# Spare bf16 products on constants between TensorE's steps, in two front ends and in the tail

## The reference, cut to what matters

```python
mod = (_silu(L0_c) @ L0_wmod).reshape(L0_c.shape[0], 6, 1, -1)
h = _layernorm(x) * (1 + ca) + sa
x = x + ga * _L0_attn_ref(h, ...)
h = _layernorm(x) * (1 + cb) + sb
x = x + gb * _L0_ffn_ref(h, ...)
# inside _L0_attn_ref, per pair of names:
scores = (relu(x @ modr_w1 + modr_b1) @ modr_w2 + modr_b2)      # top 128 of the 256 tokens, in order
n1 = _ln(tok);  uv = n1 @ m_in_w;  u, res = halves of uv         # a gated mix
tok = tok + (u * s * silu(res)) @ m_out_w
n2 = _ln(tok);  logits = n2 @ moe_r_w + moe_r_b                  # top 2 of 8 experts
h1 = gelu(n2 @ moe_w1[e] + moe_b1[e]);  eo = h1 @ moe_w2[e] + moe_b2[e]
# inside _L0_ffn_ref: both operands of each product are rounded to 8 magnitudes in blocks of 16
h = silu(fp4_linear(x, w_gate)) * fp4_linear(x, w_up);  out = fp4_linear(h, w_down)
```

## Time and profile before

| | |
|---|---|
| median of 3 runs | 287.74 us (287.31 to 289.43) |
| the profiled execution's own time | 289.48 us |
| its span, first to last instruction | 287.8 us |
| mean clock granted to TensorE over the span | 0.788 of full |
| busy: PE, PEld, DVE, ACT, POOL | 186.8, 149.6, 182.0, 111.2, 104.5 us |
| DMA | 30.74 MB, 107 GB/s in the mean |

### The profile page before, as it was taken

One profiled execution on the slowest core, in us unless ns is written; L12 is line 12 of the kernel. 1 busy time (PEld: TensorE's weight loads), 2 busy tenths in 40 slices (PEclk: granted clock), 3 DMA queues, 4 the chain that ended last, 5 costly groups with the idle time before them and its releaser, 6 DMA issues.

```text
span 287.8 us, 3751 instructions
## 1 busy us (share of the span) xinstructions
PE 186.8 (65%) x1079; PEld 149.6 (52%) x1079; DVE 182.0 (63%) x569; ACT 111.2 (39%) x321; POOL 104.5 (36%) x120
## 2 busy tenths in 40 slices
PE   2574578893337599887999679399798560083630
PEld 1321563742336469776578667298777460041530
DVE  0994856277887845693498466998568216879510
ACT  2426213143502264860457456446556400022210
POOL 6400037110641871057011615845304378300370
PEclk9957595786559597996699999989999875559575
DMA  7920002000117940466139564628284021000000
GB/s 214 331 76 0 0 2 55 18 1 1 36 61 274 370 131 2 146 187 202 54 85 292 189 216 130 192 94 259 67 282 127 28 56 46 9 0 0 2 27 9
DMA packets 22964, 30.74 MB, mean 107 GB/s; under 512 B 2128, under 2 KB 16792, under 8 KB 22944
## 3 DMA queue, kind: packets, MB, share of 16 engines
q1 hardware_dynamic: 20896, 26.30, 29.0%
q0 software_dynamic: 2048, 4.20, 4.8%
HBM read 24.45 MB, written 6.05 MB: 106 GB/s over the span
## 4 chain that ended last, share of the span: by engine, by line
PE 36%; DVE 27%; POOL 11%; issue 9%; ACT 9%; DMA 3%; SPq 1%; DVEq 0%; ACTq 0%; POOLq 0%
PE aux_ps L1083 20%; PE moe_ps L1083 7%; POOL ys L498 3%; POOL hx L466 3%; ACT hT L590 3%; POOL xs_dram L491 3%; PE small_ps L1083 2%; DVE q_am L757 2%; DMA hx<-x_dram 2%; PE aux_ps L1284 2%; DVE stats L726 2%; DVE hh L1055 2%; DVE hh L1051 1%; DVE qa L771 1%; PE aux_ps L1110 1%
## 5 line engine op out<-in xcount | busy, mean ns | idle before, releaser
L654 ACT ACTIVATE h1T<-moe_ps,w_e 128x128 f32<-128x128 f32 x120 | 33.9, 375 | 12.7 <-PE moe_ps L1083 10.3
L1083 PE MATMUL moe_ps<-xsT,w_e 128*128 128x128 f32 x240 | 32.8, 282 | 7.0 <-issue 6.7
L1083 PEld LDWEIGHTS moe_ps<-xsT,w_e 128*128 128x128 f32 x240 | 30.0, 196 | 9.1 <-issue 8.3
L1083 PE MATMUL moe_ps<-w_e,h1T 128*128 128x128 f32 x240 | 33.7, 289 | 1.7 <-ACT h1T L654 1.7
L1083 PEld LDWEIGHTS moe_ps<-w_e,h1T 128*128 128x128 f32 x240 | 30.8, 201 | 3.7 <-ACT h1T L654 2.5
L477 POOL TENSOR_TENSOR rstd<-veps,half_pow 128x4 f32<-128x4 f32 (+2 forms) x11 | 12.3, 1116 | 52.1 <-DVE veps L731 51.9
L491 POOL DMA_INDIRECT xs_dram<-xd,slot_ix x16 | 16.1, 1005 | 26.7 <-DVE slot_ix L987 22.4
L466 POOL TENSOR_TENSOR hx<-qa,q_sc 128x704 f32<-128x704 f32 (+2 forms) x6 | 7.5, 1255 | 44.3 <-DVE qa L772 44.3
L1051 DVE SCALAR_TENSOR_TENSOR hh<-gth,aux_ps 128x352 f32<-128x352 f32 x16 | 8.3, 519 | 17.4 <-ACT gth L692 17.3
L1284 PE MATMUL aux_ps<-ident,hx 128*128 128x128 f32 (+1 forms) x48 | 9.6, 354 | 14.4 <-POOL hx L466 14.4
L498 POOL DMA_INDIRECT ys<-ys_dram,slot_ix x16 | 15.9, 993 | 7.5 <-issue 4.1
(11 more groups left out here) (218 smaller groups left out, 442.5 us busy)
## 6 DMA issues: line engine op xcount, KB each, us to landing
w_e<-moe_w_dram SPq DMA_DIRECT2D x30, 514.0 KB, 4.4
mod_r<-mod_dram SPq DMA_DIRECT2D x1, 2048.0 KB, 7.6
xs_dram<-zeros SPq DMA_DIRECT2D x2, 960.0 KB, 7.5
ys<-xs_dram SPq DMA_DIRECT2D x6, 256.0 KB, 6.2
ys_dram<-ys SPq DMA_DIRECT2D x6, 256.0 KB, 2.4
hx<-x_dram SPq DMA_DIRECT2D x2, 512.0 KB, 5.8
wmod_s<-wmod_dram SPq DMA_DIRECT2D x1, 384.0 KB, 4.3
ys<-xs_dram SPq DMA_DIRECT2D x2, 192.0 KB, 7.3
```

Source lines behind the costliest of these rows:

```text
L654: last = nc.scalar.activation(h1T[:, n % 2, hc, :], moe_ps[n % MOE_BANKS][:, hc, :], ACT.Gelu, bias=w_e[:, n % WSLOTS, at:at + 1])
L1083: return nc.tensor.matmul(o, lhsT=l, rhs=r, start=start, stop=stop)
```

## The change

A new kind of step, `warm`, stands in 18 places of TensorE's order: 13 in the two front ends and 5 in the tail. In `warm.g.i` the last number isn't a part but a count: the step issues i products of the two constants, bf16, 128x128 by 128x512, into a `moe_ps` bank. With g = 0 that is bank 2, before the experts first use it, with g = 1 bank 0, once tile 27's result has been taken out of it (the wait on `ys_ready`). Nobody reads the result. The first family has 97 products, the second 76. The other engines' orders are as they were.

```diff
 ORDERS = {
     "PE": """
-        modh.0.0 modh.1.0 hT.0.0 hr.0.0 srow.0.0 scol.0.0 place.0.0 perm.0.0 mod.0.0 soft.0.0 n1.0.0 inproj.0.0
-        mix.0.0 attn.0.0 hT.1.0 hr.1.0 srow.1.0 n2.0.0 logits.0.0 slots.0.0 gateT.0.0 bias2.0.0 scol.1.0
...
+        modh.0.0 modh.1.0 warm.0.18 hT.0.0 hr.0.0 srow.0.0 warm.0.1 scol.0.0 warm.0.17 place.0.0 warm.0.3
+        perm.0.0 mod.0.0 soft.0.0 warm.0.5 n1.0.0 warm.0.1 inproj.0.0 warm.0.2 mix.0.0 attn.0.0 hT.1.0 hr.1.0
+        srow.1.0 n2.0.0 warm.0.1 logits.0.0 warm.0.11 slots.0.0 gateT.0.0 warm.0.1 bias2.0.0 scol.1.0 warm.0.16
+        place.1.0 warm.0.8 perm.1.0 soft.1.0 warm.0.13 n1.1.0 wqT.0.0 inproj.1.0 xT.0.0 mix.1.0 attn.1.0 xT.0.1
...
+        up.1.12 down.1.11 hqT.2.0 up.1.13-14 down.1.12-14 warm.1.9 hqT.2.1 dn.2.0-1 warm.1.52 h2T.3.0 gu.3.0-1
+        h2T.4.0 gu.4.0-1 warm.1.11 hqT.3.0 warm.1.3 dn.3.0 hqT.4.0 warm.1.1 dn.4.0
...
-                if kind == "modh":
+                if kind == "warm":
+
+                    pe.wait_ge(consts, 1)
+                    if g > 0:
+                        pe.wait_ge(ys_ready, NG * XT - 2)
+                    for n in range(i):
+                        mm(moe_ps[0 if g > 0 else 2][:].rearrange("p c n -> p (c n)"), before_b[:],
+                           lower[:].rearrange("p h s -> p (h s)"))
+                elif kind == "modh":
```

More of the change, by code:

```diff
@@ L63 @@
     "PE": """
-        modh.0.0 modh.1.0 hT.0.0 hr.0.0 srow.0.0 scol.0.0 place.0.0 perm.0.0 mod.0.0 soft.0.0 n1.0.0 inproj.0.0
-        mix.0.0 attn.0.0 hT.1.0 hr.1.0 srow.1.0 n2.0.0 logits.0.0 slots.0.0 gateT.0.0 bias2.0.0 scol.1.0
-        place.1.0 perm.1.0 soft.1.0 n1.1.0 wqT.0.0 inproj.1.0 xT.0.0 mix.1.0 attn.1.0 xT.0.1 up.0.0-1 xT.0.2
-        down.0.0 n2.1.0 down.0.1 logits.1.0 up.0.2 xT.0.3 up.0.3 slots.1.0 down.0.2 up.0.4 gateT.1.0 up.0.5
-        down.0.3-4 up.0.6 down.0.5 up.0.7 bias2.1.0 down.0.6 h2T.0.0 gu.0.0-2 down.0.7 up.0.8 gu.0.3 up.0.9
@@ L69 @@
[L69 to L73, removed]
@@ L74 @@
-        dn.3.0 hqT.4.0 dn.4.0
+        modh.0.0 modh.1.0 warm.0.18 hT.0.0 hr.0.0 srow.0.0 warm.0.1 scol.0.0 warm.0.17 place.0.0 warm.0.3
+        perm.0.0 mod.0.0 soft.0.0 warm.0.5 n1.0.0 warm.0.1 inproj.0.0 warm.0.2 mix.0.0 attn.0.0 hT.1.0 hr.1.0
+        srow.1.0 n2.0.0 warm.0.1 logits.0.0 warm.0.11 slots.0.0 gateT.0.0 warm.0.1 bias2.0.0 scol.1.0 warm.0.16
+        place.1.0 warm.0.8 perm.1.0 soft.1.0 warm.0.13 n1.1.0 wqT.0.0 inproj.1.0 xT.0.0 mix.1.0 attn.1.0 xT.0.1
+        up.0.0-1 xT.0.2 down.0.0 n2.1.0 down.0.1 logits.1.0 up.0.2 xT.0.3 up.0.3 slots.1.0 down.0.2 up.0.4
@@ new lines @@
+        gateT.1.0 up.0.5 down.0.3-4 up.0.6 down.0.5 up.0.7 bias2.1.0 down.0.6 h2T.0.0 gu.0.0-2 down.0.7 up.0.8
+        gu.0.3 up.0.9 down.0.8 up.0.10 hqT.0.0 down.0.9 dn.0.0 up.0.11-12 down.0.10 hqT.0.1 down.0.11 up.0.13
+        dn.0.1 down.0.12 xT.1.0 up.0.14 xT.1.1 down.0.13 up.1.0 xT.1.2 up.1.1 down.0.14 h2T.1.0 xT.1.3 gu.1.0-1
+        up.1.2 gu.1.2 down.1.0-1 up.1.3 gu.1.3 hqT.1.0 down.1.2-3 up.1.4 dn.1.0 down.1.4 up.1.5 hqT.1.1 down.1.5
+        up.1.6-7 dn.1.1 down.1.6 up.1.8-9 down.1.7-8 h2T.2.0 down.1.9 gu.2.0-2 up.1.10-11 gu.2.3 down.1.10
```

## The result

The change is faster. Beside it on the same chip the kernel before had a median of 288.59 us (4 executions, 287.31 to 291.19), the change 278.89 us (4, 276.55 to 282.00); the ratio is 0.9626, 95% interval 0.9519 to 0.9733. In two later series it had 278.78 (4) and 278.75 us (6). The ratios leave out executions over 1.5% above the fastest of the same kernel (here the one of 282.00), the medians don't, so that a ratio isn't exactly the quotient of two medians and leans on how fast the fastest happened to be. The profiled execution took 278.92 us with a span of 277.2.

The account below looks back on a forecast made before the run. No engine fills the span; a chain of waits over all engines bounds it, TensorE 36%. Held-clock terms of 6.65 us less 0.3 overrun give 6.35; 287.74 - 6.35 = 281.4, rounded to 281.3 us, range 274.5 to 287.5.

Parts of the forecast that it names:

- A product costs 0.22 us: One added bf16 product of 512 columns: 0.22 us at the full clock, 0.45 at the low one, so all runs fit.
- the 0.3 us of overrun: Charged in all for the runs of 5, 11 and 13 products, which exceed their waits at the low clock.
- within 0.2 us: Claim that using the Trainium skill's 215.7 and 426.7 ns a product would leave its sums the same within 0.2 us.
- Worth of a held clock: Time the steps in both front ends and the tail would save at the full clock: 17.2 us if everything held.
- How much is held: Shares of 0.1 to 0.65 put on each step's worth, giving 6.65 us, less 0.3 of overrun: 6.35.
- mostly lost: `inproj` and `attn` of group 0, behind narrow `soft` and `mix`: shares held only 0.2 (with `n1`) and 0.3.
- `inproj.0` still at over 5 us: Sign that the forecast is right: group 0's `inproj` keeps taking over 5 us after the change.
- The tail: `gu` of set 3, 2.5 us at share 0.1, and last `hqT`, 1.0 us at 0.4: 0.25 and 0.4 us.
- Covered overrun: 16 products ahead of `place.1`, 7.2 of 5.15 us at the low clock, cost nothing: VectorE takes its result only at 82.62.
- the clock held throughout: Rival: the full clock holds everywhere, gaining 17.2 us, 270.5; anything below 277.7 counts. Chance 0.13.
- the late TensorE: Rival: products run at 0.45 us and delay `place`, `n1`, `slots`, `n1.1` by 5.2 us, 293 or over 300. Chance 0.06.
- the forecast's case: Some steps held at the full clock and some not, 277.7 to 285 us; chance 0.60.

Follow-up runs that it names:

- front ends only: The change without the 76 products of the tail, the 97 of the front ends kept; median 278.53 us, ratio 0.9709 to the kernel before.
- full tail: The change's front ends with longer tail runs (88 products for 52, 22 for 11) and new ones ahead of `gu` of set 3 and the last `hqT`; 276.53 us.
- front 0: The kernel before with only the 59 products up to `slots` of group 0; median 285.74 us.
- fuller: The change with longer runs of products everywhere and three new ones; median 276.92 us, ratio 0.9639 to the kernel before.
- split: The full tail with 5 products ahead of `soft` of group 1, 9 instead of 13 behind it, and 2 ahead of `mix.1`; median 278.28 us.
- tail-only kernel: The kernel before with only the 76 products of the tail, none in the front ends; median 288.15 us, ratio 1.0066.
- nothing behind soft: The change without the 5, 1 and 2 products behind `soft`, `n1` and `inproj` of group 0; median 281.19 us, ratio 0.9823 to the kernel before.

## Why the prediction was right, and which step was mis-sized

The mechanism was as forecast. Its steps, by the change's profile:

- **A product costs 0.22 us**: 0.225, and 0.219 in the run of 52 (11.39 us). In this profile the filling fits everywhere but at `slots`, where 3.8 us passed in place of 3.5: the 0.3 us of overrun that was charged. In others it was more: `slots` was 1.0 us late in the change's third profile, in front ends only and in the full tail, and in the third and in the full tail the 17 products ran partly at the low clock, 5.53 us, and made `place` 0.2 us late. The 215.7 ns of the Trainium skill (TensorE: Matmul & The Clock Gate, Part 1), cited there, agree within 0.01 us. (The prediction's "within 0.2 us" holds for the sums at the high clock; at the low one its runs of 11 to 16 differ by 0.3 to 0.4.)
- **Worth of a held clock.** Foretold 3.2, 1.8 and 1.8 us for `hT` to `srow`, `perm` and `attn`. `srow` ends at 21.3 instead of 24.2 (2.9), `perm` saves 1.81, `attn` 1.73, `n1` and `inproj` 2.9 of the foretold 3.1, `perm.1` 1.67 of 1.7, `n1.1` to the end of `inproj.1` 1.9 of 2.1. These prices held; that of `gu` of set 3, 2.5 us, did not: with the clock held there, in the full tail, the next step came 0.9 us sooner.
- **How much is held**: this step failed in size. It said that `inproj` and `attn` of group 0 were "mostly lost" and gave shares of 0.65, 0.45, 0.2 and 0.3 for the first front end. Eight profiled executions have its products unchanged or longer (the change three times, front ends only, front 0, fuller, full tail, split). `hT` to `srow` and `perm` ran at full speed in all eight, `inproj` in six (3.7 us; 5.89 and 5.97 in the other two), `attn` in five. With shares of 1, 1, 0.75 and 0.6 its four terms give 3.2 + 1.8 + 2.3 + 1.1 = 8.4 us instead of 4.05; the forecast would have been 4.3 us lower, 277, a little below what was measured. In the second front end, over the seven of these profiles that have its products, `perm.1` ran at full speed in four (foretold share 0.6) and `inproj.1` in five (0.45): another 0.5 us. Less the 0.65 us that the forecast had for the tail, the forecast would still be about 277. Why 278.8 us were measured and not that stays open, apart from up to 1.0 us at `slots`. The reason behind the low shares was half right. 173 products of 8 columns gave nothing, and with nothing wide behind `soft` the clock fell. But the prediction misread the stretch from 36.4 to 43.0 us: of TensorE's 4.95 us there, `soft` and the other narrow products into `small_ps` are 2.17, and the rest of `perm`, `mod` and the transposes 2.85, so that it wasn't "mostly" one-column work. And that therefore little would be held isn't so: the eight products behind `soft`, `n1` and `inproj`, 1.8 us of work, are worth some 2.3 us. The sign "`inproj.0` still at over 5 us" accordingly didn't come: 3.70.
- **The tail**: costed at 0.65 us (0.25 for `gu` of set 3, 0.4 for the last `hqT`), measured nothing. `gu` of set 3 has 5.06 us in both. The last `hqT` was no faster, 1.54 us, and the last `dn` fell into the low clock and lost 1.3 us, in this execution; in the other two profiles of the change it took 1.58.
- **Covered overrun**: at `place.1` eight products behind it ran at the low clock, 3.35 us, and `perm.1` still waited 0.66 us for VectorE.

Of the rivals, the clock held throughout is nearest in the first front end, and the late TensorE was seen, at `slots` for 0.3 to 1.0 us and in the fuller version for 2.6. The change falls between the forecast's case and the full hold. Over the transposes of `hT` at 15.8 to 17.5 us the clock stayed at 1.00, with wide products on both sides. That such transposes don't hold it, as the Trainium skill (TensorE: Matmul & The Clock Gate, Part 4, PE-mode transpose) states, no run here tested by itself.

Left open: why the clock falls in one execution and holds in another at the same instruction. The change's first profile had `inproj` at 1.00, its second, here, at 0.50, with the same work ahead:

```profile
36.32 1.24 PE L1084 MATMUL moe_ps<-lower,before_b 128*128 128x512 bf16 x5
38.12 1.12 PE L1175 MATMUL aux_ps<-ident,xh 128*128 128x128 f32 x4 [0.56 <-DVE xh L885]
...
40.11 5.89 PE L1084 MATMUL aux_ps<-n1T,w_in_s 128*128 128x512 f32 x8 [0.44 <-ACT n1T L614]
```

Nor is it settled how much of the two fronts' joint gain is more than their sum.

## What to carry to other kernels

Where TensorE waits in short gaps on a chain that it shares with other engines, look at the granted clock under the wide steps behind each gap; if it is 0.50, wide products on constants into a bank that nobody reads buy it back, as long as the idle rest behind them is small. Fill until about a microsecond is left: half a filling had a quarter of the gain, and a rest of 8.6 us left 52 products worthless where 0.9 us left 88 and their neighbours worth some 2 us. Behind narrow products it may pay to leave more room: in one profile the clock fell there, 18 products took 6.88 instead of 4.0 us, and the next step was late. And judge such a change by many executions and several profiles, as one profile is one draw.

## What the runs showed of the hardware that was not expected

- TensorE idle for 5 us may still be granted 1.00, and the clock then falls while it is idle, not as the work comes. (That it outlasts some idleness the prediction had read from 12.0 to 15.7 us.) In the tail-only kernel the products end at 239.2 us and the next instruction starts at 247.86. In between the clock is at 1.00 up to 244.5 and at 0.50 from 245 on, 2.9 us before anything runs:

```profile
239.40:244.40 5.00, 0.00 (x0) 0.00 (x0) 4.66 (x19) 0.00 (x0) 2.55 (x4) 1.00 0.08 26
244.80:254.00 9.20, 5.67 (x10) 2.81 (x10) 7.04 (x19) 2.03 (x5) 1.17 (x2) 0.50 0.00 0
...
247.86 0.69 PE L1275 MATMUL aux_ps<-ident,hx 128*128 128x128 f32 x2 [8.67 <-POOL hx L466]
```

The kernel before shows the low clock in idleness too; its `dn` had ended at 234.8 us, and `h2T` came at 251.89:

```profile
240.00:242.00 2.00, 0.00 (x0) 0.00 (x0) 1.97 (x8) 0.00 (x0) 1.70 (x2) 0.50 0.10 33
```

- Executions of one kernel differ by where the clock falls: the kernel before ran from 283.77 to 292.46 us over 43 executions, with mean granted clocks of 0.778 to 0.830; the lower the clock, the longer the time (correlation -0.71). Two executions of other versions lie far outside: 301.80 us at a mean clock of 0.685 (tail only) and 344.71 at 0.557 (nothing behind soft). One profile of such a kernel is one draw: `slots` of group 0 started at 69.66 us in the earlier trace rows and at 65.4 us in the tail-only kernel, whose front ends are the same.
